# Four edge loops of a graph network written out batch by batch, with waits on constants and gathers that read their indices in place

## The reference

```python
# layer 0: 8 heads, softmax over the edges of a destination
alpha = leaky_relu(s[src] + s[dst], 0.2);  e = exp(alpha - segment_max(alpha, dst)[dst])
attn = segment_sum(Vh[src] * (e / segment_sum(e, dst)[dst])[:, :, None], dst)
# layer 1: 128 filters, W made from each edge's 32 radial features and a cosine cutoff
agg = segment_sum((h @ W_lin1.T)[src] * W, dst)
# layer 2: one head, softmax of a logit of node and edge features (edge_attr, 128 wide)
out = segment_sum(h[src] * softmax_over_dst(logit), dst)
# layer 3: degree-normalised sum of x @ W
out = segment_sum((x @ W)[src] * dinv[src] * dinv[dst], dst)
```

## Time and profile before

| | us |
|---|---|
| median of 3 runs (4922.61 to 4928.61) | 4924.11 |
| the profiled execution | 4921.07 |
| its span, first to last instruction | 4919.2 |
| busy in it: PE / DVE / POOL / ACT | 3538.2 / 3354.0 / 3195.0 / 2073.1 |
| POOL's 3328 gathers (L682) | 3155.9 |
| PE's 4992 matmul passes of L757 in the plain form | 1681.2 |
| DVE's 3328 adds (L769) | 1299.4 |
| mean granted clock of TensorE | 0.795 of full speed |

### The profile page before, as it was taken

How to read it: one execution, slowest core, us unless ns; L and a number is a source line. 1 busy time by engine, 2 the same in 40 slices (tenths; PEclk the granted TensorE clock), 3 DMA queues, 4 the chain that set the end, 5 groups by cost and what they waited for, 6 DMA issues and landing times. The chain is left out here.

```text
span 4919.2 us, 91583 instructions
## 1 busy us (share of the span) xinstructions
PE 3538.2 (72%) x13716; PEld 2495.3 (51%) x13717; DVE 3354.0 (68%) x9594; ACT 2073.1 (42%) x6262; POOL 3195.0 (65%) x3432
## 2 busy tenths in 40 slices
PE   6868777777799677777677578888888555555555
PEld 3545555555575455555555455555555344444443
DVE  6578888888851677777777477777777444444444
ACT  1366666666562523333333466666666100000000
POOL 0277777777300277777777577777777477777776
PEclk9977887887899878888888677777777677777777
DMA  3154555544310244444444244444444233333333
GB/s 99 53 139 137 138 138 137 138 137 137 87 46 0 82 132 124 127 125 125 126 123 113 76 111 113 112 113 112 111 110 107 66 111 111 112 112 111 111 112 99
DMA packets 345766, 537.68 MB, mean 109 GB/s; under 512 B 75816, under 2 KB 237899, under 8 KB 345675
## 3 DMA queue, kind: packets, MB, share of 16 engines
q0 software_dynamic: 146432, 386.15, 28.9%
q1 hardware_dynamic: 192187, 144.11, 10.4%
q10 hardware_dynamic: 7056, 6.48, 0.4%
HBM read 506.37 MB, written 30.07 MB: 109 GB/s over the span
## 5 line engine op out<-in xcount | busy, mean ns | idle before, releaser
L682 POOL DMA_INDIRECT e_rows<-table,e_stage x3328 | 3155.9, 948 | 1371.2 <-issue 839.4
L757 PE MATMUL banks<-e_rows,e_hot 128*128 128x273 f32 (+2 forms) x4992 | 1681.2, 472 | 732.4 <-DMA e_rows<-table,e_stage 445.7
L769 DVE TENSOR_TENSOR acc<-acc,banks 128x273 f32 (+3 forms) x3328 | 1299.4, 390 | 854.5 <-PE banks L757 641.4
L757 PEld LDWEIGHTS banks<-e_rows,e_hot 128*128 128x128 f32 x4992 | 1091.2, 250 | 1027.6 <-issue 508.2
L757 PE MATMUL banks<-e_rows,e_weighted_hot 128*128 128x257 f32 x1664 | 649.5, 523 | 31.2 <-ACT e_weighted_hot L920 28.7
L884 ACT ACTIVATE e_apart<-const,dst_loc 128x128 bf16<-128x128 f32 x1664 | 507.2, 388 | 0.1
L693 ACT COPY e_stage<-src_idx 128x8 int32 (+1 forms) x416 | 79.3, 193 | 1009.1 <-DMA e_rows<-table,e_stage 983.5
L757 PEld LDWEIGHTS banks<-e_rows,e_weighted_hot 128*128 128x128 f32 x1664 | 362.8, 246 | 130.5 <-ACT e_weighted_hot L920 42.7
L1011 PE MATMUL banks<-reach,const 64*128 (+1 forms) x416 | 100.2, 317 | 241.5 <-DVE e_tops L1147 241.4
L920 ACT ACTIVATE e_weighted_hot<-e_hot,e_weight 128x128 f32<-128x128 f32 x832 | 254.3, 388 | 16.4 <-ACT e_weight L915 14.7
L1576 DVE TENSOR_TENSOR e_hot<-banks,dst_loc 128x1024 f32<-128x1024 f32 x208 | 253.2, 1217 | 0.1
(11 more groups left out here) (314 smaller groups left out, 4885.0 us busy)
## 6 DMA issues: line engine op xcount, KB each, us to landing
e_edge_in<-in_edge_attr SPq DMA_DIRECT2D x832, 80.0 KB
e_rows<-table,e_stage POOLq DMA_INDIRECT x3328
e_node_rows<-node_line SPq DMA_DIRECT2D x104, 256.0 KB, 3.6
table<-n_row SPq DMA_DIRECT2D x49, 132.0 KB, 1.7
table<-fn_row ACTq DMA_DIRECT2D x49, 129.0 KB
X<-in_x SPq DMA_DIRECT2D x1, 6272.0 KB, 22.6
values<-table SPq DMA_DIRECT2D x49, 128.0 KB, 2.0
table<-gn_row SPq DMA_DIRECT2D x49, 128.0 KB
```

The lines of the kernel that those rows point to most:

```text
L682: nc.gpsimd.indirect_dma_start(out=rows[:, u, q, 0:width], out_offset=None, in_=table, in_offset=bass.IndirectOffsetOnAxis(ap=stage[:, u, ...
L757: nc.tensor.matmul(banks[:, 2 + q % turn, 0:width], onehot, rows, start=True, stop=True).then_inc(summed_tile, 1)
L769: nc.vector.tensor_tensor(at, at, banks[:, 2 + q % turn, 0:width], ALU.add).then_inc(added, 1)
```

## The change

All loops over batches are written out: every batch's number is a constant, so thresholds and slices are too. Registers that were kept over a loop's edge are gone; each batch's blocks are still loaded. A gather takes its indices as a column of `src_idx`, so `e_stage`, its semaphore and ACT's copies are gone, and its wait stands on the DMA. The node work behind the loops, and the stages between, are as they were.

```diff
-def turns(nc, engine, body, peeled=0):
-    ...
-    with nc.Fori(peeled, TURNS - 1, engines=[engine], head_slot={engine: 0}) as i:
-        for r in range(RING):
-            body(i * RING + r, r)
-    for r in range(RING):
-        body((TURNS - 1) * RING + r, r)
+def turns(body):
+    for n in range(BATCHES):
+        body(n, n % RING)

-def node_turns(nc, engine, body):
-    ...
+def node_turns(body):
+    def rank(n):
+        return (n - LAG) // 2 if n >= LAG else None
+    for n in range(BATCHES):
+        body(n, n % RING, rank(n), rank(n - 2))

             def gather(n, u):
-                pool.wait_ge(staged, n + 1)
-                pool.sem_inc(carriers, 1)
                 for q in range(G):
                     pool.wait_ge(summed_tile, summed(n - RING, q))
-                    pool.sem_inc(carriers, 1)
+                    at = src_idx[:, n * G + q:n * G + q + 1]
                     nc.gpsimd.indirect_dma_start(out=rows[:, u, q, 0:width], out_offset=None, in_=table,
-                                                 in_offset=bass.IndirectOffsetOnAxis(ap=stage[:, u, q:q + 1], axis=0)).then_inc(gathered[u], 16)
+                                                 in_offset=bass.IndirectOffsetOnAxis(ap=at, axis=0)).then_inc(gathered[u], 16)

-        def stage_indices(act, n, u, stage, staged, gathered):
-            if later(n, RING - 1):
-                act.wait_ge(gathered[u], arrived(n - RING, u))
-            nc.scalar.copy(stage[:, u, :], src_idx[:, bass.ds(n * G, G)]).then_inc(staged, 1)

         class RowAhead:
-            ...
+            def read(self, n):
+                if not inside(n):
+                    return
+                self.blocks = nc.values_load_multi_w_load_instructions(batch_row[0:1, bass.ds(n, 1), 0:self.count]...)[1]

                         def batch(j, r, k=None, last=None):
-                            if inside(j + RING):
-                                stage_indices(act, j + RING, r, stage, staged, gathered)
```

More of the change, by code:

```diff
@@ L705, in build, with __init__ @@
         class RowAhead:
-            def __init__(self, tag, count):
+            def __init__(self, count):
                 self.count = count
[L709 to L721, removed]
+                self.read(0)
+            def read(self, n):
                 if not inside(n):
                     return
[L724 to L733, removed]
+                self.blocks = nc.values_load_multi_w_load_instructions(
+                    batch_row[0:1, bass.ds(n, 1), 0:self.count].squeeze(1), engines=[DVE_ENGINE], min_val=0, max_val=NB - 1,
+                    skip_runtime_bounds_check_because="clamped when they were made")[1]
         def load_ranked(engine, k):
@@ L829, in _ @@
                     def _(pool):
-                        gather_batches(pool, table, row_w, rows, stage, staged, gathered, summed_tile)
+                        gather_batches(pool, table, row_w, rows, gathered, summed_tile)
                     @blk.sync
@@ L858, in _ @@
                             load_rows(1, 1)
-                            turns(nc, SP_ENGINE, batch)
+                            turns(batch)
                         else:
@@ L863, in _ @@
                             load(1, 1)
-                            node_turns(nc, SP_ENGINE, batch)
+                            node_turns(batch)
                             for k in range(IN_LOOP - 1, NB):
@@ L971, in _ @@
                         if many:
-                            turns(nc, ACT_ENGINE, batch)
+                            turns(batch)
                         else:
                             node.act_start(act)
-                            node_turns(nc, ACT_ENGINE, batch)
+                            node_turns(batch)
                             for k in range(IN_LOOP - 1, NB):
@@ L1079, in _ @@
                         if many:
-                            turns(nc, PE_ENGINE, batch)
+                            turns(batch)
                         else:
                             node.pe_start(pe)
-                            node_turns(nc, PE_ENGINE, batch)
+                            node_turns(batch)
                             for k in range(IN_LOOP - 1, NB):
@@ L1313, in batch @@
                                 tile_maxima(j + 2, r % 2)
-                        ahead = RowAhead(tag, G if many else ROW_REGS)
+                        ahead = RowAhead(G if many else ROW_REGS)
                         if many:
-                            turns(nc, DVE_ENGINE, batch)
+                            turns(batch)
                         else:
                             node.dve_start(dve)
-                            node_turns(nc, DVE_ENGINE, batch)
-                        ahead.end()
+                            node_turns(batch)
                         if not many:
@@ L1371, in _ @@
                     def _(pool):
-                        gather_batches(pool, table, width, rows, stage, staged, gathered, summed_tile)
+                        gather_batches(pool, table, width, rows, gathered, summed_tile)
                     if not filtered:
@@ L1397, in load @@
                                     sp.dma_start(edge_in[:, u, q, :], inp["edge_attr"][bass.ds(tiles[q] * P, P), :]).then_inc(edge_ready[u], 16)
-                            turns(nc, SP_ENGINE, load)
+                            turns(load)
                             for u in range(RING):
@@ L1452, in batch @@
                                 keep_scaledT(j + 2, r % 2)
-                        if not filtered:
-                            turns(nc, ACT_ENGINE, batch)
-                        else:
+                        if filtered:
                             node.act_start(act)
-                            node_turns(nc, ACT_ENGINE, batch)
+                            node_turns(batch)
                             node.act_store(act, IN_LOOP - 1)
@@ L1627, in batch @@
                                 one_hot(j + 1, un)
-                            ahead.read(j + 1, u)
+                            ahead.read(j + 1)
                             add(2)
@@ L1648, in batch @@
                             add(7)
-                        ahead = RowAhead(tag, ROW_REGS)
-                        node_turns(nc, DVE_ENGINE, batch)
-                        ahead.end()
+                        ahead = RowAhead(ROW_REGS)
+                        node_turns(batch)
                         if filtered:
```

40 lines of the change are left out of this document (8 added, 32 removed).

## The result

The changed kernel takes 4897.35 us (median of 4 runs, 4893.86 to 4899.66), the kernel before 4923.36 (4919.64 to 4928.61): ratio 0.9949, 95% interval 0.9938 to 0.9961, 26.0 us less by the medians. Forecast were 4886 and a range of 4860 to 4921. A repeat on chip 15 gave 0.9941 (0.9924 to 0.9957). The profiled execution has a span of 4897.7 us, 21.5 less than before.

The account below looks back on a forecast made before the run. POOL's gathers at 1.25 us each were taken as the bound, with consumers lagging in the first and third stages. Gains of 15.8 (first), 20.6 (third) and 0.8 each (second, fourth) sum to 38.0 us: 4886, range 4860 to 4921.

Parts of the forecast that it names:

- Bound and supply: POOL's gathers at 1.25 us each, eight a batch, supply about 10.0 us a batch, and cannot be passed.
- Part 1, the gathers: All stages: dropping semaphore instruction, register arithmetic and index copies is worth 0, bounds 10 us gain or loss.
- Rival (d): The 0.305 us gap before gathers is partly the semaphore instruction: 250 us gained in second and fourth stages, 4636; chance 0.05.
- Part 2, starts: First gathers of stages come earlier: 4.7 us in the first stage, 0.8 us in each of three others.
- Part 3 in the third stage: Written-out consumers (DVE, PE, ACT) keep step with gathers: 7.0 us of ring waits and 12.8 us of lag gained.
- ring and lag: Third stage: gathers' waits for a free ring place, 7.0 us, and growth of the consumers' lag, 14.3 down to 1.5.
- The reserve: Third stage: written-out consumers need 9.1 us a batch against 10.0 supplied, so DVE waits about 1 us a batch for rows.
- Part 3 in the first stage: Written-out consumers just keep step with gathers: 3.6 us of ring waits gone, lag growth 11.2 down to 3.7 us.
- half the batches each: 10.05: First stage: batches of 9.5 and 10.6 us, half each, give a mean just under the supply of 10.09.
- rival (a): First and third stages: PE's granted clock holds the pace, so half of the consumers' gain is lost, about 4908; chance 0.22.
- the 4908: Time forecast if PE's clock takes back the consumers' gain: 22 us gained with half lost, 6 with all lost.
- Rival (b): DVE and PE, first and third stages: written-out code is fetched all the time, 104 us of misses, 4990; chance 0.08.

Follow-up runs that it names:

- s7_all_written_copies: Kernel before with all edge-stage loops written out, but ACT's index copies and the separate waits before gathers kept: 4895.60 us, ratio 0.9947.

## Why the prediction was right, and where it was wrong

**Bound and supply: right.** A gather takes 1.25 to 1.26 us in every stage, in loops and out of them.

**Part 1, the gathers, value 0: right** within some 8 us, by s7_all_written_copies: 0.9947 beside 0.9949. Rival (d) is ruled out by the gaps, which are 0.305 us without the semaphore instruction as with it.

**Part 2, starts: right in size for the first stage** (5.42 to 0.71, 4.7 foretold). The 0.8 us at each of the three others came only as 1.2 in front of the fourth stage; in front of the second and third the stretch from last add to first gather grew by 1.65 and 1.0 us in code that wasn't changed. Why is open. All written-out kernels on quick chips show the first of these, 1.4 to 3.3 us; it builds up steadily over the stretch's first 230 us and not at one place. The second is 1.0 to 1.1 us in the changed kernel, its repeat and the one with eight more products, and 0.0 to 0.3 in the other three.

**Part 3 in the third stage: right in the main.** 17.1 us of the 19.8 foretold for ring and lag: ring waits gone, lag 29.1 where some 27 was foretold (26.8 in the repeat). L2174's wait for the registers' load stayed, 30.5 us in 44 times, 0.69 each. The reserve was overrated: the prediction took 9.1 us a batch from one written-out turn, and expected DVE to wait 1 us a batch for rows; it waits 0.3. Short and long batches alternate in this stage too, as before.

**Part 3 in the first stage: wrong, and this is the step that failed.** The prediction had the two batch lengths right, 9.5 and 10.6, and then wrote "half the batches each: 10.05". The share of batches at half clock was taken as a constant of the stage. It isn't: it rose from a half to two thirds, and the mean stayed at 10.25. The stage gave 6.8 us of 15.8. Between the two profiled executions the gain is 21.5 us of the 38.0 forecast, 16.5 short: 9.0 here, 4.5 in the third stage and the stretch ahead of it, 2.75 in the second and the stretch ahead of it, and 0.35 ahead of all stages (the fourth gave 0.1 more than forecast). The prediction's own signs said so: lag 41.6 at clock 0.74 was its sign of rival (a), and 3.0 us of idle beyond the gaps its sign that part 3 is wrong. Rival (a) named the mechanism and priced it for both stages; of the 11.1 us that it put at stake in the first, 9.0 were lost, and in the third few. By its own sum, half of part 3 lost is 4902 and all of it 4917; the 4908 lies between. That 4897 fell into the range is thanks to the third stage, and to bounds that took (a) in; for the first stage the central sum was not borne out.

Why the stages differ: in the first a short batch (9.5) is under the supply only by 0.6, and a long one (10.6) over it by 0.5, so that a rise of the share of long ones takes the whole gain. In the third the share stayed at a half, and the mean fell to 10.065. Why the share rose in the first stage is open. That PE became idler in the shorter batches is not borne out: in short batches at the full clock it was busy for 6.4 of 9.6 us before and for 6.3 of 9.5 after. Shown by the added products is that more work for PE holds its clock, and that the stage then keeps step with the gathers. That it was PE's idle time which cost it the clock agrees with this, and is a reading.

The Trainium skill's page "Runtime: NRT & Kernel Launch", section "Instruction fetch mechanics", says that straight code is fetched ahead with the cost mostly hidden. The trace agrees for the edge stages: 369 packets, and 0.9 us of unexplained gaps before the first stage's adds. Rival (b) had no part there. That every edge of these loops would be a fetch was the prediction's own step; no run tells whether the head of a loop was still loaded at its edge.

## What to carry to other kernels

When two engines share a pace and one of them has a clock that is granted, don't hold the share of slow stretches fixed while shortening the other's work: count after the change how many batches are slow. Here the share rose from a half to two thirds and took the gain back, and filling PE's idle time with work nobody needs was then 8 to 10 us faster, where 30 us less of DVE's work was worth nothing that could be measured. And look at the kernel's supply first: two of four stages had nothing to win, and the trace said so in one row.

## What the runs showed of the hardware that was not expected

- Some 1660 added PE instructions raised the granted clock of a stage from 0.74 to 0.97 and made the kernel 8 to 10 us faster.
- The same kernel took 4922 to 4926 us on chips 2 and 15 and 6156 to 6181 on chips 9, 11 and 12. In the profiles of kernels like it from both, gathers took 946 to 950 ns on POOL. On the slower chips waits between engines stood 2 to 4 us after the work they waited for had ended. The cause is open.
- On such a chip written-out loops are worth 4.7%, on the others 0.5%.
- With the clock at 0.97 gathers of that stage lasted 965 ns on POOL, though nothing of theirs was changed; they took 953 to 957 in it in every other profile from a quick chip.
- The granted clock did not give the length of a batch: 9.62 us at 0.82 in the kernel before, 10.4 to 10.5 at 0.84 with the maxima turned earlier.
